# Rotary attention: the partner elements of each rotation by crosswise transfers between partitions, in place of a second projection

## What is computed

```
Q = (x @ W_q)  16 heads of 16;   K, V = x @ W_k, x @ W_v   4 heads of 16
for each pair (x0, x1) = elements (2i, 2i+1) of a head:
    r0 = x0 * cos - x1 * sin
    r1 = x0 * sin + x1 * cos
scores = Qr Kr^T / 4;  out = softmax(scores) V;  x = x + out @ W_o
```

## Time and profile before

| | us |
|---|---|
| three runs: median (lowest to highest) | 1550.89 (1548.24 to 1556.73) |
| the profiled execution | 1558.22 |
| its span, first to last instruction | 1556.4 |
| mean granted TensorE clock | 0.947 |
| busy: TensorE, weight loads, VectorE, ScalarE, GpSimd | 1384.5, 971.4, 1088.5, 621.3, 329.6 |

### The profile page before, as it was taken

How to read it: one execution, slowest core, us unless ns; L and a number is a source line. 1 busy time by engine, 2 the same in 40 slices (tenths; PEclk the granted TensorE clock), 3 DMA queues, 4 the chain that set the end, 5 groups by cost and what they waited for, 6 DMA issues and landing times. The chain is left out here.

```text
span 1556.4 us, 20758 instructions
## 1 busy us (share of the span) xinstructions
PE 1384.5 (89%) x7632; PEld 971.4 (62%) x7632; DVE 1088.5 (70%) x2216; ACT 621.3 (40%) x1156; POOL 329.6 (21%) x291
## 2 busy tenths in 40 slices
PE   5799999788999989999977999999799889889797
PEld 4455555477888878888851333323377668677676
DVE  5756566498679568887648666676376578888865
ACT  2255545453333333333223555566532334334221
POOL 4211100072433304433322131200022001021010
PEclk9799999799999999999986999999899999999899
DMA  7828330120000000000043250400000000000000
GB/s 153 95 30 109 47 38 2 35 93 1 1 1 1 1 1 1 1 1 1 1 52 57 43 79 28 66 2 1 1 0 1 0 1 0 1 1 1 14 14 27
DMA packets 32319, 39.05 MB, mean 25 GB/s; under 512 B 6002, under 2 KB 27226, under 8 KB 32090
## 3 DMA queue, kind: packets, MB, share of 16 engines
q1 hardware_dynamic: 32218, 37.73, 14.4%
HBM read 14.45 MB, written 2.10 MB: 11 GB/s over the span
## 5 line engine op out<-in xcount | busy, mean ns | idle before, releaser
L1370 DVE TENSOR_REDUCE attn_negm<-ps 128x2 f32<-128x1024 f32 (+3 forms) x256 | 260.2, 1024 | 94.6 <-PE ps L977 53.3
L1190 ACT ACTIVATE attn_probs<-ps 128x512 f32<-128x512 f32 (+3 forms) x512 | 236.8, 515 | 156.3 <-PE ps L1005 82.7
L501 POOL TENSOR_TENSOR moe_h_low<-expert_h,moe_h_high 128x512 fp32r<-128x512 f32 x96 | 137.6, 1435 | 271.4 <-ACT moe_h_high L446 271.4
L997 PE MATMUL ps<-attn_qs,attn_ks 99*128 99x512 bf16 (+4 forms) x512 | 154.3, 352 | 30.3 <-ACT attn_probs L1190 19.4
L977 PE MATMUL ps<-attn_ks,attn_qs 96*128 96x512 bf16 (+4 forms) x512 | 143.6, 364 | 16.9 <-DVE attn_negm L1370 14.8
L464 ACT ACTIVATE moe_silu<-ps 128x512 f32<-128x512 f32 x96 | 57.4, 598 | 200.5 <-PE ps L366 200.2
L1817 PE MATMUL ps<-sb_f_down,tail_h 128*128 128x256 f32 x512 | 122.9, 386 | 7.2 <-DVEq L2108 7.2
L997 PEld LDWEIGHTS ps<-attn_qs,attn_ks 102*128 102x128 bf16 (+1 forms) x512 | 43.9, 98 | 132.2 <-ACT attn_probs L1190 101.1
L1018 PE MATMUL ps<-attn_probs,attn_va 128*32 128x512 f32 (+3 forms) x1024 | 119.6, 541 | 0.0
L1817 PEld LDWEIGHTS ps<-sb_f_down,tail_h 128*128 128x128 f32 x512 | 98.0, 192 | 24.1 <-DVEq L2108 7.3
L2081 DVE TENSOR_TENSOR tail_h<-tail_silu,ps 128x512 f32<-128x512 f32 x64 | 43.6, 682 | 86.1 <-PE ps L1807 54.0
(11 more groups left out here) (350 smaller groups left out, 3252.8 us busy)
## 6 DMA issues: line engine op xcount, KB each, us to landing
attn_qs<-attn_part SPq DMA_DIRECT2D x96, 128.0 KB, 4.6
attn_ks<-attn_part SPq DMA_DIRECT2D x48, 128.0 KB, 7.3
out_x<-x SPq DMA_DIRECT2D x4, 512.0 KB, 2.6
attn_ks<-attn_part SPq DMA_DIRECT2D x24, 64.0 KB, 4.4
x<-in_x SPq DMA_DIRECT2D x2, 512.0 KB, 4.4
x<-in_x SPq DMA_DIRECT2D x1, 1024.0 KB, 10.3
moe_raw<-in_f_down SPq DMA_DIRECT2D x2, 512.0 KB, 6.4
sb_f_gate<-in_f_gate SPq DMA_DIRECT2D x2, 512.0 KB, 4.6
```

Of the source, the lines that this page charges most:

```text
L501: pool.tensor_tensor(hc.low[:, j % RING, :], h[:, j % RING, :], hc.high[:, j % RING, :], ALU.subtract).then_inc(low_done, 1)
L997: last = pe.matmul(ps[:, SC + k, 0:width2(kt)], ks[0:ROWS2, b % 2, hd % KH, kt * P:(kt + 1) * P], qs[0:ROWS2, b % 2, hd, T - width2(kt):T] ...
L1190: act.activation(pr[:, s2 % RING, j, 0:n], ps[:, SC + k, 0:n], ACT.Exp, scale=HD ** -0.5).then_inc(exp_done, 1)
L1370: dve.tensor_reduce(m, ps[:, 2 * half:2 * half + 2, 0:width1(qt)], AX, ALU.max, negate=True).then_inc(r1_free, 1)
```

## The change

The swapped weights, their splits and the swapped products go. Each chunk is projected once per image and copied by ScalarE from PSUM to a new buffer `raw` (three slots, TURNS). The dimensions of a head are laid out with the even ones first and the odd ones behind, so that partners lie half a chunk apart; SP issues two transfers a chunk that exchange the halves from `raw` to `rot` (64 x 512 float32 each, 32 x 512 for k0). VectorE multiplies `raw` by cos, now from SBUF and after ScalarE's copy. The multiply by sin waits for both transfers: on VectorE for image 0 (where the copy of the next chunk and its multiply by cos are put ahead of a chunk's rotation), on GpSimd for the others. The product stands in the middle of its step; the high parts stay two steps behind. On SP the swaps of image 1 come before the last stack of image 0, and those of images 2 and 3 before the maxima transfer of the unit in which they are projected. The bank is emptied by ScalarE. The constants are permuted to the new order, and `swapped` goes.

```diff
@@ attention: lists @@
     def projections(b):
         for k, ch in enumerate(CHUNKS):
-            parts = ["plain"] if causal else ["plain", "swapped"]
-            for m, part in enumerate(parts):
-                yield k, m, ("project", b, ch, part)
+            yield k, 0, ("project", b, ch)
...
     for k, m, job in projections(0):
         early.append(job)
-        if not causal and m == 1:
-            early += [("high", 0, job[2]), ("low", 0, job[2])]
+        if not causal and k > 0:
+            early += [("high", 0, CHUNKS[k - 1]), ("low", 0, CHUNKS[k - 1])]
+    if not causal:
+        early += [("high", 0, CHUNKS[-1]), ("low", 0, CHUNKS[-1])]
...
-        if kind in ("rows", "flip", "out") or kind == "project" and (causal or job[3] == "plain" or job[1] == 0):
+        if kind in ("rows", "flip", "out") or kind == "project" and causal:
             return "dve"
...
-        names = ["wq", "wk", "wv"] if causal else ["wq", "wq2", "wk", "wk2", "wv"]
+        names = ["wq", "wk", "wv"]
...
-            qk, rot = s.sb("qk", [P, NCH, T]), s.sb("rot", [P, 2, T])
+            qk, raw, rot = s.sb("qk", [P, NCH, T]), s.sb("raw", [P, TURNS, T]), s.sb("rot", [P, TURNS, T])
@@ sync @@
+            def swap(b, k):
+
+                i, n = NCH * b + k, rows_of[CHUNKS[k]]
+                sp.wait_ge(free["act"], jobs.count[("project", b, CHUNKS[k])])
+                at_least(sp, turned, i - TURNS + 1)
+                for to, at in ((0, n // 2), (n // 2, 0)):
+                    sp.dma_start(rot[to:to + n // 2, i % TURNS, :], raw[at:at + n // 2, i % TURNS, :]).then_inc(swapped_in[i % TURNS], 16)
...
+            if not causal:
+                for k in range(NCH):
+                    swap(0, k)
             for k in range(NCH):
+                if not causal and k == NCH - 1:
+                    for i in range(NCH):
+                        swap(1, i)
                 stacks(0, k)
             later = iter(load_later)
             for b in range(B):
                 for grp in range(4):
+                    if not causal and grp == 0 and 2 <= b + 1 < B:
+                        for k in range(NCH):
+                            swap(b + 1, k)
                     maxima(4 * b + grp)
@@ scalar: project @@
-                elif kind == "swapped" and b > 0:
-                    at_least(act, turned, NCH * b + k - 1)
+                else:
+                    at_least(act, turned, NCH * b + k - TURNS + 1)
                     act.wait_ge(ready, jobs.number[job])
-                    act.activation(rot[0:n, k % 2, :], ps[0:n, jobs.bank[job], :], ACT.Copy).then_inc(free["act"], 1)
+                    act.activation(raw[0:n, (NCH * b + k) % TURNS, :], ps[0:n, jobs.bank[job], :], ACT.Copy).then_inc(free["act"], 1)
@@ gpsimd: turn @@
-                pool.wait_ge(free["act"], jobs.count[("project", b, ch, "swapped")])
-                pool.tensor_tensor(rot[0:n, k % 2, :], rot[0:n, k % 2, :], sin[0:n, :], ALU.mult).then_inc(rotated, 1)
-                pool.wait_ge(free["dve"], jobs.count[("project", b, ch, "plain")])
-                pool.wait_ge(rotated, NCH * (b - 1) + k + 1)
-                pool.tensor_tensor(qk[0:n, k, :], qk[0:n, k, :], rot[0:n, k % 2, :], ALU.add).then_inc(turned, 1)
+                i = NCH * b + k
+                pool.wait_ge(swapped_in[i % TURNS], 32 * (i // TURNS + 1))
+                pool.tensor_tensor(rot[0:n, i % TURNS, :], rot[0:n, i % TURNS, :], sin[0:n, :], ALU.mult).then_inc(rotated, 1)
+                pool.wait_ge(scaled, i + 1)
+                pool.wait_ge(rotated, i + 1)
+                pool.tensor_tensor(qk[0:n, k, :], qk[0:n, k, :], rot[0:n, i % TURNS, :], ALU.add).then_inc(turned, 1)
@@ vector: project, turned0 @@
-                    dve.wait_ge(ready, jobs.number[job])
-                    dve.tensor_tensor(qk[0:n, k, :], ps[0:n, jobs.bank[job], :], w["cos" + ch[0]][0:n, :],
-                                      ALU.mult).then_inc(free["dve"], 1)
-                elif b == 0:
-                    dve.wait_ge(ready, jobs.number[job])
-                    dve.tensor_tensor(rot[0:n, k % 2, :], ps[0:n, jobs.bank[job], :], w["sin" + ch[0]][0:n, :],
-                                      ALU.mult).then_inc(free["dve"], 1)
+                    dve.wait_ge(free["act"], jobs.count[job])
+                    dve.tensor_tensor(qk[0:n, k, :], raw[0:n, (NCH * b + k) % TURNS, :], w["cos" + ch[0]][0:n, :],
+                                      ALU.mult).then_inc(scaled, 1)
...
-                dve.wait_ge(free["dve"], jobs.count[("project", 0, ch, "swapped")])
-                dve.tensor_tensor(qk[0:n, k, :], qk[0:n, k, :], rot[0:n, k % 2, :], ALU.add).then_inc(turned, 1)
+                dve.wait_ge(swapped_in[k], 32)
+                dve.tensor_tensor(rot[0:n, k, :], rot[0:n, k, :], w["sin" + ch[0]][0:n, :], ALU.mult).then_inc(rotated, 1)
+                dve.wait_ge(rotated, k + 1)
+                dve.tensor_tensor(qk[0:n, k, :], qk[0:n, k, :], rot[0:n, k, :], ALU.add).then_inc(turned, 1)
@@ constants @@
-    return np.array([HD * h + d for d in range(HD) for h in range(heads)])
+    return np.array([HD * h + d for d in [*range(0, HD, 2), *range(1, HD, 2)] for h in range(heads)])
```

More of the change, by code:

```diff
@@ L727, in attention @@
     SC, CTX, MISC = 4, 6, 7
+    TURNS = 3
     CHUNKS = ["q0", "k0", "q1", "k1"] if causal else ["q0", "k0", "q1"]
@@ L829, in attention @@
         xh_ready, high_ready, low_ready = s.sem("xh_ready"), s.sem("high_ready"), s.sem("low_ready")
-        rotated, turned = s.sem("rotated"), s.sem("turned")
+        rotated, turned, scaled = s.sem("rotated"), s.sem("turned"), s.sem("scaled")
+        swapped_in = [s.sem(f"swapped{k}_in") for k in range(TURNS)]
         stack_loaded, m_loaded = [s.sem("stack_loaded0"), s.sem("stack_loaded1")], s.sem("m_loaded")
@@ L942, in wait_rows, with project @@
                 pe.wait_ge(free["dve"], jobs.count[job])
-            def project(b, ch, kind):
-                wt = cut["w" + ch[0] + ("2" if kind == "swapped" else "")]
-                pe.wait_ge(w_low, names.index("w" + ch[0] + ("2" if kind == "swapped" else "")) + 1)
+            def project(b, ch):
+                wt = cut["w" + ch[0]]
+                pe.wait_ge(w_low, names.index("w" + ch[0]) + 1)
                 n = rows_of[ch]
                 f0 = P * int(ch[1])
-                bank = take_bank(("project", b, ch, kind))
+                bank = take_bank(("project", b, ch))
                 wait_rows(b)
@@ L1229, in projected @@
                 stacked(pool, b)
-                pool.wait_ge(free["dve"], jobs.count[("project", b, ch, "plain")])
+                pool.wait_ge(free["dve"], jobs.count[("project", b, ch)])
                 split_rest(b, ch)
@@ L1247, in _ @@
             for job in early:
-                if not causal and job[0] == "project" and job[3] == "swapped":
+                if not causal and job[0] == "project":
                     turn(job[1], job[2])
@@ L1413, in _ @@
             for job in early:
-                if causal and job == ("project", 0, "q1", "plain"):
+                if causal and job == ("project", 0, "q1"):
                     dve.wait_ge(x1_in, 16)
@@ L2281, in rows @@
     return np.ascontiguousarray(w.reshape(w.shape[0] // P, P, w.shape[1]).transpose(1, 0, 2))
-def swapped(w):
-    return w.reshape(w.shape[0], -1, 2)[:, :, ::-1].reshape(w.shape)
 def laid_out(v):
@@ L2309, in laid_out @@
         "f0_de": rows(v["L0_ffn_down_embed"].T), "f0_ue": rows(v["L0_ffn_up_embed"]),
-        "a1_wq": rows(v["L1_attn_a_W_q"][:, order]), "a1_wq2": rows(swapped(v["L1_attn_a_W_q"])[:, order]),
-        "a1_wk": rows(v["L1_attn_a_W_k"][:, four]), "a1_wk2": rows(swapped(v["L1_attn_a_W_k"])[:, four]),
+        "a1_wq": rows(v["L1_attn_a_W_q"][:, order]), "a1_wk": rows(v["L1_attn_a_W_k"][:, four]),
         "a1_wv": rows(v["L1_attn_a_W_v"]), "a1_wo": rows(v["L1_attn_a_W_o"]),
```

13 lines of the change are left out of this document (7 added, 6 removed).

## The result

Twenty executions of each kernel on one chip gave a median of 1555.31 us before and 1549.07 us after: ratio 0.9957, 95% interval 0.9939 to 0.9974. By the ratio that is 6.7 us less; the two medians lie 6.2 us apart. The forecast was 10.2 us less, from 1550.9 to 1540.7. The kernel before had a median of 1550.89 us in its first three runs and 1555.31 in twenty, so the ratio is what counts, and not the absolute time: 0.9957 is 6 to 7 us. By the prediction's own bound of 0.5% that is no change, with an interval that reaches over the bound.

A forecast was written before the change was run, and what follows sets the result against it. TensorE, busy for 89% of the span, was taken as the bound. A head gain of 2.0 us plus 8.2 for images 2 and 3 made 10.2 us less, from 1550.9 to 1540.7 us, range 1534 to 1549.

The forecast's parts named there:

- B: Rival: freed slots fill with waits, transfer pair landing at 5.0 us, VectorE 0.5 later; gain 4.1 us, 1546.8; chance 0.24.
- The four steps: Sign of being right: image 2's four projection steps take 20 to 20.5 us in place of 24.35.
- Head: Start of the rotary stage, up to image 0's scores: 2.0 us gained in sum, between 0.3 and 4.2.
- The start: Head: ScalarE splits two weights fewer, so TensorE starts 0.6 us earlier, at 782.1.
- The chain: Head: VectorE's rotation chain of image 0 ends at 802.0 instead of 801.1, 0.9 us lost.
- Image 1's projections: Head: 18 matmuls instead of 36, 13 taken as slow, 6.7 us, 2.9 gained; with six slow 5.3 and 4.3 gained.
- Removed: Images 2 and 3, each: swapped slots 4.4 us, merge wait 0.9, exponentials wait 0.6; sum 5.9 us gained.
- (a): Images 2 and 3, steps 17 to 19: ScalarE's copies delay the exponentials; 0.3 us lost per image for all three.
- (b): Images 2 and 3: longer way to "turned" through copy, transfer pair and GpSimd; ScalarE waits 1.0 us for q1 per image.
- (c): Images 2 and 3: cos multiply with two SBUF inputs is held beside GpSimd; 0.5 us lost per image.
- A: Rival: transfers land near 2.0 us, every high part timely; gain 16.0 us, 1534.9; chance 0.22.
- C: Rival: transfer is the stage's clock, ScalarE waiting at steps 19 to 21; at pair L = 10, 8 us slower, 1559; chance 0.06.

The follow-up runs named there:

- spread: Changed kernel with images 2 and 3 projected at steps 1, 3, 5 instead of 1, 2, 3; ratio 0.9946 to the kernel before.
- early_rows: Changed kernel with image 0's values and image 1's transposes ahead of k0's high part in the head; ratio 0.9892 to the kernel before.
- the second profile: Changed kernel run and profiled again without any edit; ratio 0.9957 to the kernel before.
- psum_cos: Changed kernel with the multiply by cos reading PSUM again, TensorE waiting for it before reusing the bank; ratio 0.9896 to the kernel before.
- before_copy: Kernel before plus ScalarE's copies of the plain projections in images 1 to 3, cos still reading PSUM; ratio 1.0002 to the kernel before.
- psum_late: psum_cos with an unused transfer awaited before every pair of images 2 and 3; ratio 0.9915 to the kernel before.
- sbuf_k0: psum_cos with only chunk k0's multiply by cos, images 1 to 3, reading SBUF again; ratio 0.9907 to the kernel before.

## Why the prediction was wrong

**The forecast** was 10.2 us less and 0.66 for faster by over 0.5%; it is 6.7 us less, in the case of no change. The measured gain is within the range in relative terms (its low end of gain was 1.9 us); the absolute median of 1549.07 is just above its upper edge of 1549. The nearest case is B, at 0.24: the freed slots fill with waits. But of its two halves only one did it, VectorE held by GpSimd; the transfers, 2.7 us of B's price per image, were quicker than even the forecast had them. That B's 4.1 us lie near the measured 6.7 is luck. Of the signs that the prediction names for being wrong two came: landings below 2.5 us, and multiplies by cos of 1.61 and 1.78 us with TensorE waiting. The four steps took 18.4 us, where 20 to 20.5 were named as right.

**Head.** Its sum, 2.0 us, was met (2.04); its parts less so. The start is not 0.6 us earlier but the same (3.62 and 3.58 us behind the split; only in the profiles of spread and early_rows, which leave that stretch as it is, is it 0.6 earlier). The chain ends 0.65 us later, near my 0.9, but not through the transfer, which k0's projection covers. Two errors offset each other there: the start came 0.6 us later than forecast, and from it to the multiply by sin it was 0.8 us less. Image 1's projections take 6.93 us with 13 slow matmuls, as I had it (6.7). The 13 is luck: I took it from "some 10 us of little work" ahead of 782.72, but TensorE had worked without a break until 776.3, 6.4 us before. In the second profile seven of them were slow, 5.7 us, and the head gained 3.6: the other price of the text, "with six it is 5.3 and 4.3 gained". A single profile shows one of the two, and the length of the wait does not tell which: seven were slow behind a wait of 10.95 us, 13 behind 9.82.

**Removed, 5.9 us per image.** Right: 5.95 from the windows, 5.96 with nothing else in the way (psum_cos). No merge waits, and TensorE waits 0.38 us at 895.95 in place of 0.85.

**(a) The copies, 0.3 us.** They cost nothing (before_copy).

**(b) The wait for q1's turned, 1.0 us.** The mechanism is right, the term was mis-sized: a pair takes 2.9 us and not 3.9, and by the step's own formula, pair minus 2.9, the wait is then zero. It was. The row of 3.3 us that I took was the nearest in kind and wrong by 1 us. The Trainium skill, DMA: Bandwidth & Descriptors, in the section on the anatomy of one DMA, gives about 2.0 us fixed plus the bytes at 436 GB/s. That makes an estimate of 2.3 us for such a transfer, and the 2.3 of the tile agrees.

**(c) The multiply by cos, 0.5 us.** This is the step that failed. I had the mechanism, the right row for its size (1.02 in place of 0.18) and "each may wait 1.3 us with the row maximum behind it". Measured were 0.9 to 1.1 where it was held. What I priced wrongly is what stands behind it: "there are 1 to 2 us of room before TensorE needs that". That room was read from the old steps, in three of which a swapped slot of up to 1.5 us still stood. In the new ones VectorE has 0.9 us of idle time ahead of q1's multiply (0.19 once k0's is long too), and the maxima split, four more instructions that can meet GpSimd, comes right after. Its casts of 0.62 and 1.02 us stood in the trace of the kernel before, at this very place, and the sum has no term for them. The term is 4.8 us per image, 2.4 of waits and 2.45 of clock, or 2.4 where the clock holds. With 4.8 for (c) and zero for (a) and (b), an image gives 5.95 - 4.8 = 1.15 us and the whole 2.0 + 2.3 = 4.3; where the clock holds in both images it is 9.1. The measured 6.7 (4.0 to 9.5 by its interval) lies between.

**Rival B's 0.5** for VectorE was called the least that rule and row allow. That sentence was right, and I should have followed it to the next instruction. **A** did not happen in the change as it is. psum_cos comes near it: its gain, 0.0104 of 1553, is 16 us, where A had 16.0. The images gave what A had (5.96 and 6.1 us for its 5.9), the head did not (2.0 for its 4.2), so part of that agreement is luck: from the first weight split to the last context matmuls psum_cos is 15.8 us shorter. **C** was off: L is 2.9, and in psum_late 3.5 us more cost 2.9 and 2.2, no more than C's slope.

## What to carry to other kernels

When an edit moves an operand of a VectorE instruction from PSUM to SBUF, price the instructions behind it in the schedule as it will be, not as it is: the slack there is one of the things that the edit takes away. Where another engine must copy a tile out of PSUM anyway, the second reader may still read the bank, at the price of one wait for whoever reuses it. And where an instruction takes longer than its twins and ends together with one of another engine, here GpSimd's, that is a sign of who holds it, even where the trace shows no wait.

## What was unexpected of the hardware

The hold works both ways: the engine that starts second is the one that waits. VectorE's multiply took 1.61 us in place of 0.69 when it started second, and GpSimd's instruction 1.76 in place of 1.27 or 1.64 in place of 1.15 when it did. So a shift of 0.1 us decides which engine pays: k0's multiply took 1.78 us when it started 0.03 us behind GpSimd's instruction (889.27 and 889.24, changed kernel), and 0.68 when it started 0.05 us ahead (878.28 and 878.33, sbuf_k0).

The same stall of TensorE, 1.2 us of work in 3.6, was followed by a granted clock of 0.50 for 6.4 us in one execution and by 1.00 in another of the same kernel. This doubles the price of the stall, from 2.4 to 4.85 us, and makes single profiles of one kernel differ by several microseconds. Two intervals of the output steps (26 to 28) do the same without any edit: 6.37 and 6.46 us in image 2 of the kernel before, 6.03 and 5.20 in its image 3; no edit accounts for them, and they are in the times of the whole stage. The stage, from the first weight split to the last context matmuls, took 324.5 and 318.1 us in two profiles of the changed kernel.
